# Weight means moved from ScalarE to VectorE and into the attention stage, and the softmax epilogue spread over the next tile

## The chip, the cores and the metric

One Trainium2 chip, all 8 cores, one launch. Two cores share one sequence of the batch of four: each computes 2048 of its 4096 rows of the output (blocks of 512 rows, taken alternately), and repeats the keys and values of the whole sequence for itself. There is no exchange between cores. The metric is the device time of the slowest core, in microseconds (us).

## What is computed

A pre-norm transformer layer on x of 4 x 4096 x 2048: `x1 = x + Attention(LN(x))`, then `x1 + FFN(LN(x1))`. Attention has 16 heads of 128, rotary positions and a causal mask. The FFN is a gated one with ternary weights:

```python
def _weight_quant(w):
    scale = jnp.clip(jnp.mean(jnp.abs(w)), EPS, None)
    wq = jnp.clip(jnp.round(w / scale), -1.0, 1.0) * scale
    return w + jax.lax.stop_gradient(wq - w)
...
gate = _bitlinear(x, w_gate)
up = _bitlinear(x, w_up)
return _bitlinear(jax.nn.silu(gate) * up, w_down)
```

What matters here is `mean(abs(w))` of three weight matrices of 64 MB each. A whole matrix must be read for its mean before its first element can be quantized, so the kernel reads 192 MB for the three means, long before the FFN reads the same matrices again.

## The kernel before

Each of the five engines (TensorE = PE, VectorE = DVE, ScalarE = ACT, GpSimd = POOL, SyncE = SP) works through its own list of instructions in order; the lists are recorded in program order and replayed (`Rec.replay`, so that every instruction of the trace carries line 68). A DMA sits in the list of the engine that issues it. Where an instruction waits for a semaphore, everything behind it in that engine's list waits too. The helpers `vop`, `sop` and `gop` also make each operation wait for the one before it on its own engine.

The stages, one after the other, with a barrier of all engines between them:

1. Rotary tables and the first layer norm. 2. Projections of q, k and v. 3. Attention (`with ExitStack() as p2`). 4. Output projection, x1 and the second norm (`p3`). 5. Gate and up matmuls with ternarizing (`p4`). 6. Down matmul (`p4e`).

**The weight means** (`wa_chunk`, L566). The 192 MB are cut into 192 chunks of 128x2048 f32 (1 MB). A chunk is loaded by a DMA that POOL issues into one of two tiles, `wa_t0` and `wa_t1`; POOL waits until the chunk that was in the tile before has been read. ACT then runs `Abs` over the chunk with its sum accumulated into `wa_tmp`, and a second instruction of one column adds that to `wa_acc`. `wa_feed(n)` (L592) puts n chunks at the place where it is called: 6 behind each of the 16 heads (L815), 4 in each of the 16 tiles of the output projection (L893), and 2 in each of the 16 tiles of the second pass over x1 (L937). `wa_epilogue` (L597), behind that pass, turns the three sums into the thresholds that stage 5 needs.

**Attention.** A head has four query tiles of 512 (`t`), and tile t has K_t = 8(t+1) key blocks of 128 (`kb`), 80 blocks in all. For each block PE makes the scores (`pb <- p_qT,p_kT`) in one of three PSUM banks, ACT the exponential into `p_E`, and DVE multiplies the last eight blocks of each tile by the mask. `drain` (L751) then adds the block to the row sums (`p2S <- p_E,g_ones_colb`) and to the context (`pb <- p_E,p_v`, in pb2 or pb3 by the parity of t); it runs three blocks behind the scores. `p2S` is one bank for all tiles. At the end of each tile the list reads:

```python
while pending2:
    p_ = pending2.pop(0)
    drain(p_, p_[0] == 0)
avdone = (sT, sT.v)
wait(V, avdone, (sV, sV.v))
vop("reciprocal", invr[:], p2S[0:1, :])
```

so the three blocks that are left are drained first. Then follow the reciprocal of the row sums on one partition (DVE), its broadcast to 128 partitions by an f32 matmul (PE, `p2A`), the copy out of PSUM (ACT, `p_bcb`), the product with the context (DVE, `p_ctx`) and the store (issued by ACT). I call these five the tile's epilogue. The first score matmuls of the next tile stand behind the broadcast on PE, and its first exponential stands behind the store on ACT.

**Between two heads.** At the end of head h stand 6 chunks on ACT (L815). At the start of head h+1 `load_head` (L661) has SP load q, k and v of head h+2 (2.5 MB, into the tiles that head h has given up), and `normB` (L681) makes the bound that head h+2 subtracts in its exponentials: DVE squares q and k (`p_dump`), PE sums them over the partitions in 12 matmuls, DVE takes 12 maxima (`p_nm`), and ACT, DVE and PE combine them into `p_negB`. The scores of head h+1 stand behind all of that in PE's list.

**Output projection** (L850). For each of 16 tiles of 128 rows: 64 matmuls in four PSUM banks, 8 DVE additions, then on ACT the store of x1 and two passes with accumulated sums (`p_dump`), then on DVE two reductions for the largest and the smallest value (`p_sw`), which wait for ACT's passes. The second pass (L920) loads x1 again and quantizes it with five DVE operations a tile.

Of the kernel before, what the change touches and what calls it, by code (L numbers as in the profile page):

```python
# [84 lines left out]
def build_program(upto=99):  # L85
# [535 lines left out]
    with ExitStack() as p2:  # L621
# [117 lines left out]
        for h in range(NH):  # L739
# [27 lines left out]
            pending2 = []  # L767
            for t in range(4):
                K_t = 8 * (t + 1)
                for kb in range(K_t):  # L770
# [21 lines left out]
                    pending2.append((kb, t, etok))  # L792
                while pending2:
                    p_ = pending2.pop(0)
                    drain(p_, p_[0] == 0)
                avdone = (sT, sT.v)
                wait(V, avdone, (sV, sV.v))
                vop("reciprocal", invr[:], p2S[0:1, :])
                p2rel[0] = (sV, sV.v)
                wait(T, p2Arel[0], (sV, sV.v))  # L800
                top("matmul", p2A[:], g_ones_row[:], invr[:], start=True, stop=True)
                wait(Sc, (sT, sT.v))
                sop("activation", bcb[:], p2A[:], AF.Identity)
                p2Arel[0] = (sS, sS.v)
                cb = t % 2
                wait(V, (sS, sS.v), ctxrel[cb])
                vop("tensor_tensor", ctxb[cb][:], pb[2 + t % 2][:], bcb[:], ALU.mult)
                prel[2 + t % 2] = (sV, sV.v)
                wait(Sc, (sV, sV.v))
                csem[cb].inc(Sc.dma_start(  # L810
                    d_ctxT.ap()[h * 128:(h + 1) * 128, t * 512:(t + 1) * 512],
                    ctxb[cb][:]), 16)
# [534 lines left out]
```

How the kernel before makes its waits and increments, by code:

```python
    def then_inc(self, sem, val=1):  # L46
        self.incs.append((sem, val))
        return self
# [17 lines left out]
    def replay(self, eng):  # L66
        for meth, a, k, inst in self.ops:
            real = getattr(eng, meth)(*a, **k)
            for sem, val in inst.incs:
                real.then_inc(sem, val)
# [8 lines left out]
    def inc(self, inst, n=1):  # L79
        inst.then_inc(self.h, n)
        self.v += n
        return self.v
# [62 lines left out]
    def wait(rec, *toks):  # L145
        for sem, val in toks:
            if val > 0:
                rec.wait_ge(sem.h, val)
# [1 line left out]
    def barrier_all():  # L150
        for r in RECS:
            for s in sems:
                if s.v > 0:
                    r.wait_ge(s.h, s.v)
# [39 lines left out]
    def vop(meth, *a, **k):  # L194
        if sV.v:
            V.wait_ge(sV.h, sV.v)
        return sV.inc(getattr(V, meth)(*a, **k))
# [1 line left out]
    def sop(meth, *a, **k):  # L199
        if sS.v:
            Sc.wait_ge(sS.h, sS.v)
        return sS.inc(getattr(Sc, meth)(*a, **k))
# [1 line left out]
    def gop(meth, *a, **k):  # L204
        if sG.v:
            G.wait_ge(sG.h, sG.v)
        return sG.inc(getattr(G, meth)(*a, **k))
```

## Time and profile before

| what | value |
|---|---|
| median of 2 runs | 10006.01 us (9992.61 to 10019.41) |
| profiled execution, its own time | 10008.06 us |
| its span, slowest core (core 2) | 10006.5 us |
| spans of the 8 cores | 9926.9 to 10006.5 us |
| mean granted TensorE clock, cores 0 to 3 / 4 to 7 | 0.813 / 0.783 |
| busy share of core 2: PE, DVE, ACT, POOL | 60%, 42%, 23%, 14% |
| attention stage, core 2 | about 2434 to 4727 us |
| output projection and second pass, core 2 | about 4728 to 5376 us |

The profile is one execution, read on its slowest core. Busy time is per engine; a stage in which no engine is near full is one in which they wait for each other in turn, and only the timeline tells in which order. In the timeline a row is start, duration, engine, instruction with output and inputs, and in brackets how long its engine stood idle before it and which engine or DMA ended that.

### The profile page before, as it was taken

The numbers are of one execution on the slowest core, as the hardware profiler recorded it, in microseconds if no ns is written. First come the engines' busy times: TensorE is split into PE (matmuls) and PEld (weight loads), VectorE is DVE, ScalarE is ACT, GpSimd is POOL, SyncE is SP. The second block draws the span as 40 slices with busy tenths as digits, with TensorE's granted clock in tenths as the row PEclk, the third lists the DMA queues.
The fourth block names the chain that finished last, engine by engine and source line by source line (L and its number), as shares of the span: only waits on it lengthen the run. The fifth ranks groups of instructions, "written<-read, shape, count | busy, mean of one in ns | idle before, by whom it ended". The sixth has DMA issues, their size and how long they took to land.

```text
span 10006.5 us, 90582 instructions; the slowest of 8 cores (9926.9 to 10006.5 us)
## 1 busy us (share of the span) xinstructions
PE 6033.1 (60%) x23243; PEld 2298.0 (23%) x23698; DVE 4159.0 (42%) x4832; ACT 2311.2 (23%) x3870; POOL 1371.6 (14%) x770
## 2 busy tenths in 40 slices
PE   0006476497766667665630678878779717484847
PEld 0002122143111111111210233333333313232323
DVE  5503233222333323331353677777776451514140
ACT  3531011000555555454451000000000110101010
POOL 0001122100000000000001433333333100000101
PEclk9999799798777777777865899999998757575868
DMA  2483321332122211222886444444444123333433
GB/s 88 145 290 76 67 51 50 66 74 75 40 76 76 76 58 58 76 76 64 268 285 199 128 127 125 126 127 126 122 126 125 61 74 131 104 135 102 144 107 133
DMA packets 637658, 1115.46 MB, mean 111 GB/s; under 512 B 339954, under 2 KB 421874, under 8 KB 567282
## 3 DMA queue, kind: packets, MB, share of 16 engines
q1 hardware_dynamic: 433380, 530.71, 17.6%
q10 hardware_dynamic: 158976, 302.06, 9.4%
q0 software_dynamic: 44816, 276.88, 9.1%
q8 instruction: 224, 3.67, 0.2%
q14 instruction: 262, 2.15, 0.1%
HBM read 874.62 MB, written 218.10 MB: 109 GB/s over the span
## 4 chain that ended last, share of the span: by engine, by line
PE 32%; DVE 29%; DMA 11%; ACT 8%; issue 7%; POOL 6%; SPq 3%; ACTq 2%; DVEq 1%; another core or an unknown queue 1%; POOLq 0%
PE pb L68 25%; DVE p_cu L68 5%; PE p2S L68 4%; SPq L68 3%; DVE p_hqt L68 3%; DVE t_w L68 3%; DMA wa_t<-wdT 3%; POOL p_wdtb L68 3%; ACTq L68 2%; DVE p_wf L68 2%; DVE p_pm L68 2%; DVE p_invr L68 2%; ACT wa_dump L68 2%; DMA wa_t<-wuT 2%; DVE p_ht L68 2%
## 5 line engine op out<-in xcount | busy, mean ns | idle before, releaser
L68 PE MATMUL pb<-p_wgt,p_xiT 128*128 128x512 bf16 x4014 | 1080.0, 427 | 604.1 <-DVE p_ht L68 415.1
L68 PE MATMUL pb<-p_wds,p_hTg 128*128 128x512 bf16 x4009 | 1018.1, 421 | 101.6 <-DMA p_wds<-wdtd 85.3
L68 ACT ACTIVATE p_E<-pb,p_negB 128x512 bf16<-128x512 f32 x1280 | 879.8, 687 | 351.3 <-PE pb L68 118.9
L68 DVE TENSOR_TENSOR p_cu<-g_sxinv,p4a_swn 128x1 f32<-128x1 f32 x256 | 753.8, 2945 | 27.8 <-DVE p_cg L68 1.5
L68 PEld LDWEIGHTS pb<-p_wgt,p_xiT 128*128 128x128 bf16 x4096 | 430.0, 107 | 1235.9 <-issue 930.8
L68 ACT ACTIVATE p_sg<-pb,p_cg 128x512 f32<-128x512 f32 x256 | 175.9, 687 | 2211.3 <-DVE p_cu L68 1288.5
L68 DVE TENSOR_TENSOR p_E<-p_E,p_masks 128x512 bf16<-128x512 bf16 x512 | 218.0, 426 | 1056.2 <-ACT p_E L68 1054.7
L68 PE MATMUL pb<-k_pp_xT,k_pp_W 128*128 128x512 bf16 x2007 | 467.0, 384 | 297.8 <-ACT k_pp_qb L68 193.3
L68 PE MATMUL pb<-p_qT,p_kT 128*128 128x512 bf16 x1222 | 535.9, 455 | 138.5 <-ACT p_E L68 126.5
L68 PE MATMUL ptb<-g_ident,p_hqo 128*128 128x128 bf16 x1024 | 127.4, 299 | 787.1 <-DVE p_hqo L68 642.7
L68 PEld LDWEIGHTS pb<-p_wds,p_hTg 128*128 128x128 bf16 x4096 | 432.4, 106 | 683.5 <-issue 499.6
L68 PE MATMUL pb<-q_pp_xT,q_pp_W 128*128 128x512 bf16 x1003 | 230.7, 382 | 543.9 <-DMA q_pp_xT<-xlnq 456.6
L68 DVE TENSOR_SCALAR p_hqt<-p_hq,p_st 128x1024 f32<-128x1024 f32 x128 | 97.3, 760 | 1047.1 <-PE ptb L68 911.2
L68 PE MATMUL p2S<-p_E,g_ones_colb 128*1 128x512 bf16 x1280 | 523.5, 409 | 11.3 <-ACT p_E L68 3.7
L68 PE MATMUL pb<-p_E,p_v 128*128 128x512 bf16 x1258 | 528.2, 420 | 0.0
L68 PE MATMUL pb<-v_pp_W,v_pp_xT 128*128 128x512 bf16 x2007 | 442.1, 380 | 105.5 <-DMA v_pp_xT<-xlnkv 103.4
L68 PE MATMUL p4b<-p_wut,p_xiT 128*128 128x512 bf16 x2007 | 474.9, 388 | 2.4
L68 PE MATMUL pb<-p_wut,p_xiT 128*128 128x512 bf16 x2007 | 473.7, 387 | 2.4
L68 ACT ACTIVATE wa_dump<-wa_t 128x2048 f32<-128x2048 f32 x192 | 366.7, 1910 | 447.5 <-DMA wa_t<-wdT 167.6
L68 POOL TENSOR_TENSOR p_wdtb<-p_wf,p_pm 128x2048 bf16<-128x2048 f32 x64 | 289.7, 4526 | 785.7 <-DVE p_wf L68 754.0
L68 POOL TENSOR_TENSOR p_ob<-p_ev,p_x1i 128x512 f32<-128x512 f32 x64 | 90.9, 1420 | 2014.0 <-ACT p_ev L68 1929.9
L68 PE MATMUL pb<-p_Wo,p_ct 128*128 128x512 bf16 x1003 | 248.6, 410 | 176.1 <-DVE p_x L68 87.6
(169 smaller groups left out, 6799.3 us busy)
## 6 DMA issues: line engine op xcount, KB each, us to landing
wa_t<-wgT POOLq DMA_DIRECT2D x64, 1024.0 KB, 6.1
wa_t<-wuT POOLq DMA_DIRECT2D x64, 1024.0 KB, 6.7
wa_t<-wdT POOLq DMA_DIRECT2D x64, 1024.0 KB, 8.2
p_wf<-wdT SPq DMA_DIRECT2D x64, 1024.0 KB, 5.7
p_wf<-wgT SPq DMA_DIRECT2D x64, 1024.0 KB, 5.8
p_wf<-wuT SPq DMA_DIRECT2D x64, 1024.0 KB, 5.4
hfpd<-p_ht ACTq DMA_DIRECT2D x256, 256.0 KB, 3.1
p_wds<-wdtd SPq DMA_DIRECT2D x64, 1024.0 KB, 6.5
```

What stands on the lines that cost most here:

```text
L68: real = getattr(eng, meth)(*a, **k)
```

## The change

Four edits:

- `wa_chunk`: the sum of absolute values of a chunk is made by DVE (`tensor_reduce` with absolute values, then an addition of one column), no longer by ACT. Each chunk also waits for all earlier DVE work. The tile `wa_dump` is gone.
- The chunks behind a head become 12 instead of 6. With 16 heads these are all 192, so that none are left in stage 4; `wa_feed` is taken out of both its passes, and `wa_epilogue` moves to the start of stage 4, behind the issue of the load of Wo.
- The three blocks left over at the end of a tile are drained only for the last tile of a head. For the others they stay in `pending2` and are drained between the first scores of the next tile.
- The epilogue of a tile becomes four functions e1 (reciprocal), e2 (broadcast), e3 (copy) and e4 (product and store), of which one is called at each of the key blocks 3, 4, 5 and 6 of the next tile. For the last tile of a head that is the first tile of the next head, behind the 12 chunks and `normB`.

```diff
@@ wa_chunk
-        toks = [(sem, sem.v)]
+        toks = [(sem, sem.v), (sV, sV.v)]
...
-        sop("activation", wa_dump[:, :W], wa_tile[slw][:, :W], AF.Abs,
-            accum_out=wa_tmp[:])
-        wa_state["rel"][slw] = (sS, sS.v)
-        sop("activation", wa_acc[mi][:], wa_tmp[:], AF.Identity,
-            bias=wa_acc[mi][:], scale=1.0)
+        wait(V, *toks)
+        vop("tensor_reduce", wa_tmp[:], wa_tile[slw][:, :W], AX.X, ALU.add,
+            apply_absolute_value=True)
+        wa_state["rel"][slw] = (sV, sV.v)
+        wait(V, (sV, sV.v))
+        vop("tensor_tensor", wa_acc[mi][:], wa_acc[mi][:], wa_tmp[:], ALU.add)
@@ attention, for each key block
                     qk_tok = sT.v
+                    if kb >= 3 and eitems:
+                        eitems.pop(0)()
                     while len(pending2) >= 3:
@@ attention, at the end of each tile
-                while pending2:
-                    p_ = pending2.pop(0)
-                    drain(p_, p_[0] == 0)
...
+                def mk_epi(h, t, cb):
+                    def e1():
+                        wait(V, (sT, sT.v), (sV, sV.v))
+                        vop("reciprocal", invr[:], p2S[0:1, :])
+                        p2rel[0] = (sV, sV.v)
+                    def e2():
+                        wait(T, p2Arel[0], (sV, sV.v))
+                        top("matmul", p2A[:], g_ones_row[:], invr[:],
+                            start=True, stop=True)
...
+                if t == 3:
+                    while pending2:
+                        p_ = pending2.pop(0)
+                        drain(p_, p_[1])
+                eitems.extend(mk_epi(h, t, t % 2))
             hrel[sl] = (sT, sT.v)
-            wa_feed(6)
+            wa_feed(12)
@@ stage 4
+        wa_feed(len(wa_items))
+        wa_epilogue()
...
-            wa_feed(4)
...
-            wa_feed(2)
-        wa_feed(len(wa_items))
-        wa_epilogue()
```

Where e1 stands, its wait `(sT, sT.v)` counts the scores of key block 3, which PE has just been given; the drain behind it starts the row sums of the new tile in `p2S` and waits for the reciprocal (`p2rel`).

DVE's list between heads 0 and 1, before: the last masked block of head 0, its reciprocal and context, then the squares and maxima of `normB(2)`.

```order
L68 TENSOR_TENSOR p2_E7<-p2_E7,p2_masks 128x512
L68 RECIPROCAL p2_invr<-p2S 1x512
L68 TENSOR_TENSOR p2_ctx1<-pb3,p2_bcb 128x512
L68 TENSOR_TENSOR p2_dump<-p2_qT0 128x2048
L68 TENSOR_REDUCE p2_nm0<-pb5 1x1
L68 TENSOR_TENSOR p2_dump<-p2_kT0 128x4096
L68 TENSOR_REDUCE p2_nm2<-pb0 1x1
```

DVE's list at the same place now, from the last two chunks on. Ten more pairs like these stand ahead of them, behind the last masked block; `wa_t0` and `wa_t1` are the two chunk tiles.

```order
L68 TENSOR_REDUCE wa_tmp<-wa_t0 128x1
L68 TENSOR_TENSOR wa_acc0<-wa_acc0,wa_tmp 128x1
L68 TENSOR_REDUCE wa_tmp<-wa_t1 128x1
L68 TENSOR_TENSOR wa_acc0<-wa_acc0,wa_tmp 128x1
L68 TENSOR_TENSOR p2_dump<-p2_qT0 128x2048
L68 TENSOR_REDUCE p2_nm0<-pb5 1x1
L68 TENSOR_TENSOR p2_dump<-p2_kT0 128x4096
L68 TENSOR_REDUCE p2_nm2<-pb0 1x1
```

The reciprocal and the context of head 0's last tile are no longer here, and `normB(2)` stands behind twelve chunks.

DVE's list a little later, at the start of head 1:

```order
L68 TENSOR_TENSOR p2_E0<-p2_E0,p2_masks 128x512
L68 TENSOR_TENSOR p2_E1<-p2_E1,p2_masks 128x512
L68 TENSOR_TENSOR p2_E2<-p2_E2,p2_masks 128x512
L68 RECIPROCAL p2_invr<-p2S 1x512
L68 TENSOR_TENSOR p2_E3<-p2_E3,p2_masks 128x512
L68 TENSOR_TENSOR p2_E4<-p2_E4,p2_masks 128x512
L68 TENSOR_TENSOR p2_E5<-p2_E5,p2_masks 128x512
L68 TENSOR_TENSOR p2_ctx1<-pb3,p2_bcb 128x512
L68 TENSOR_TENSOR p2_E6<-p2_E6,p2_masks 128x512
L68 TENSOR_TENSOR p2_E7<-p2_E7,p2_masks 128x512
L68 RECIPROCAL p2_invr<-p2S 1x512
```

The reciprocal at the fourth row belongs to the last tile of head 0, and so does `p2_ctx1`; the one at the end belongs to the first tile of head 1.

PE's list from the first tile of head 0 into the second, before: the last two blocks are drained, the broadcast follows, then four score matmuls (into pb0, pb1, pb4, pb0) before the first drain of the new tile.

```order
L68 MATMUL p2S<-p2_E6,g_ones_colb 1x512
L68 MATMUL pb2<-p2_E6,p2_v0 128x512
L68 MATMUL p2S<-p2_E7,g_ones_colb 1x512
L68 MATMUL pb2<-p2_E7,p2_v0 128x512
L68 MATMUL p2A<-p2_invr,g_ones_row 128x512
L68 MATMUL pb0<-p2_qT0,p2_kT0 128x512
L68 MATMUL pb1<-p2_qT0,p2_kT0 128x512
L68 MATMUL pb4<-p2_qT0,p2_kT0 128x512
L68 MATMUL pb0<-p2_qT0,p2_kT0 128x512
L68 MATMUL p2S<-p2_E0,g_ones_colb 1x512
L68 MATMUL pb3<-p2_E0,p2_v0 128x512
```

And now, from the same drains on:

```order
L68 MATMUL p2S<-p2_E6,g_ones_colb 1x512
L68 MATMUL pb2<-p2_E6,p2_v0 128x512
L68 MATMUL pb4<-p2_qT0,p2_kT0 128x512
L68 MATMUL p2S<-p2_E7,g_ones_colb 1x512
L68 MATMUL pb2<-p2_E7,p2_v0 128x512
L68 MATMUL pb0<-p2_qT0,p2_kT0 128x512
L68 MATMUL p2S<-p2_E0,g_ones_colb 1x512
L68 MATMUL pb3<-p2_E0,p2_v0 128x512
L68 MATMUL pb1<-p2_qT0,p2_kT0 128x512
L68 MATMUL p2A<-p2_invr,g_ones_row 128x512
L68 MATMUL p2S<-p2_E1,g_ones_colb 1x512
L68 MATMUL pb3<-p2_E1,p2_v0 128x512
```

The drains of the old tile stand between the scores of the new one. The reciprocal runs on DVE between the scores into pb0 and the drain of `p2_E0` that follows them; the broadcast stands one block later.

## Rows read from the trace of the kernel before

**Rows 1.** DVE timeline, the last two reciprocals of one head and the first of the next: start us, us, engine, instruction, [idle before <-releaser]
```profile
2720.91 3.35 DVE L68 RECIPROCAL p_invr<-p2S 1x512 f32<-1x512 f32 x1 [1.19 <-PE pb L68]
...
2758.64 3.35 DVE L68 RECIPROCAL p_invr<-p2S 1x512 f32<-1x512 f32 x1 [1.19 <-PE pb L68]
...
2805.39 3.35 DVE L68 RECIPROCAL p_invr<-p2S 1x512 f32<-1x512 f32 x1 [1.19 <-PE pb L68]
```

**Rows 2.** ACT timeline inside a tile in steady running, one of 1280 exponentials
```profile
2604.36 0.69 ACT L68 ACTIVATE p_E<-pb,p_negB 128x512 bf16<-128x512 f32 x1 [0.16 <-ACT p_E L68]
```

**Rows 3.** PE timeline, the broadcast matmul behind a reciprocal
```profile
2584.77 2.04 PE L68 MATMUL p2A<-p_invr,g_ones_row 1*128 1x512 f32 x2 [3.74 <-DVE p_invr L68]
```

**Rows 4.** windows after it: stretch, us, busy PE, PEld, DVE, ACT, POOL, PEclk, DMA share, GB/s
```profile
2584.80:2588.30 3.50, 3.40 (x5) 0.72 (x5) 0.50 (x1) 0.60 (x1) 0.00 (x0) 0.50 0.00 0
...
2594.20:2598.00 3.80, 3.64 (x14) 0.88 (x14) 0.00 (x0) 2.96 (x5) 0.00 (x0) 1.00 0.00 0
```

**Rows 5.** timeline of the boundary between two heads, all engines
```profile
2768.97 0.53 POOL L68 DMA_DIRECT2D wa_t<-wgT  x1 [116.22 <-ACT wa_acc L68]
...
2772.19 1.23 DVE L68 TENSOR_TENSOR p_dump<-p_qT 128x2048 bf16<-128x2048 bf16 x1 [6.34 <-DMA p_kT<-kTd]
...
2777.30 1.91 ACT L68 ACTIVATE wa_dump<-wa_t 128x2048 f32<-128x2048 f32 x1 [6.02 <-DMA wa_t<-wgT]
...
2790.45 0.15 DVE L68 TENSOR_TENSOR p_nm<-p_nm 1x1 f32<-1x1 f32 x1
...
2791.74 0.55 ACT L68 ACTIVATE p_nm<-p_nm 1x1 f32<-1x1 f32 x2
...
2793.94 0.27 PEld L68 LDWEIGHTS pb<-p_qT,p_kT 128*128 128x128 bf16 x2
...
2796.64 0.59 PE L68 MATMUL p2S<-p_E,g_ones_colb 128*1 128x512 bf16 x1 [0.19 <-issue]
```

**Rows 6.** timelines of DVE, ACT and POOL behind the last head, where no head is loaded
```profile
4697.35 3.35 DVE L68 RECIPROCAL p_invr<-p2S 1x512 f32<-1x512 f32 x1 [1.19 <-PE pb L68]
...
4704.64 0.33 ACTq L68 DMA_DIRECT2D ctxTd<-p_ctx  x1
...
4707.67 0.53 POOL L68 DMA_DIRECT2D wa_t<-wuT  x1 [112.96 <-ACT wa_acc L68]
...
4715.34 0.53 POOL L68 DMA_DIRECT2D wa_t<-wuT  x1 [4.65 <-ACT wa_acc L68]
...
4726.17 0.29 ACT L68 ACTIVATE wa_acc<-wa_tmp,wa_acc 128x1 f32<-128x1 f32 x1
```

**Rows 7.** DVE timeline, output projection, from its first tile's reduction to its last
```profile
4813.53 2.29 DVE L68 TENSOR_REDUCE p_sw<-p_x 128x1 f32<-128x2048 f32 x1 [4.91 <-ACT p_dump L68]
...
4818.45 0.69 DVE L68 TENSOR_TENSOR p_x<-pb,g_bob 128x512 f32<-128x512 f32 x1 [0.17 <-DVE p_sw L68]
...
5168.93 0.18 DVE L68 TENSOR_SCALAR p_sw<-p_sw 128x16 f32<-128x16 f32 x1 [11.39 <-ACT wa_acc L68]
```

**Rows 8.** DVE timeline, second pass over x1, first two tiles and the end
```profile
5179.21 1.34 DVE L68 TENSOR_SCALAR p_tq<-p_x,p_sw 128x2048 f32<-128x2048 f32 x1 [5.25 <-DMA p_x<-x1d]
...
5188.26 1.34 DVE L68 TENSOR_SCALAR p_tq<-p_x,p_sw 128x2048 f32<-128x2048 f32 x1 [0.25 <-DVE p_xi L68]
...
5376.14 0.16 DVE L68 RECIPROCAL p4a_invtau<-p4a_tau 128x1 f32<-128x1 f32 x1 [1.61 <-ACT p4a_tau L68]
```

**Rows 9.** windows, the output projection: columns as in rows 4
```profile
4790.00:5169.00 379.00, 248.51 (x1003) 105.50 (x1022) 161.81 (x161) 211.11 (x256) 33.52 (x64) 0.83 0.86 282
```

**Rows 10.** POOL, DVE and ACT timelines, a chunk issued beside a DVE reduction
```profile
4952.59 2.29 DVE L68 TENSOR_REDUCE p_sw<-p_x 128x1 f32<-128x2048 f32 x1 [0.17 <-DVE p_sw L68]
4952.61 0.53 POOL L68 DMA_DIRECT2D wa_t<-wuT  x1 [6.36 <-ACT wa_acc L68]
...
4960.21 1.91 ACT L68 ACTIVATE wa_dump<-wa_t 128x2048 f32<-128x2048 f32 x1 [1.24 <-DMA wa_t<-wuT]
```

**Rows 11.** DMA issues of the third weight matrix: xcount, KB each, median us to landing
```profile
wa_t<-wdT POOLq DMA_DIRECT2D x64, 1024.0 KB, 8.2
```

More of the change, by code:

```diff
@@ L599, in wa_epilogue @@
             b_swn, b_tau, b_invtau = wstats[mi]
-            wait(T, prel[5], (sS, sS.v))
+            wait(T, prel[5], (sS, sS.v), (sV, sV.v))
             top("matmul", pb[5][0:1, 0:1], wa_acc[mi][:], g_ones_col[:],
@@ L675, in build_program @@
         Erel = [(sS, 0)] * NEB
+        pending2 = []
+        eitems = []
         ctxrel = [(dm["c0"], 0), (dm["c1"], 0)]
@@ L751, in drain @@
             def drain(pend, first_sum):
-                pkb, pt, etok = pend
+                pkb, pt, etok = pend[0] if isinstance(pend[0], tuple) else pend
                 eb = pkb % NEB
@@ L765, in drain @@
                 Erel[eb] = (sT, sT.v)
-            pending2 = []
             for t in range(4):
@@ L791, in build_program @@
                         etok = (sV, sV.v)
-                    pending2.append((kb, t, etok))
-                while pending2:
-                    p_ = pending2.pop(0)
[L795 to L812, printed above, removed]
@@ L813, in build_program, with e3, e4 @@
-                ctxrel[cb] = (csem[cb], csem[cb].v)
-            hrel[sl] = (sT, sT.v)
-            wa_feed(6)
+                    pending2.append(((kb, t, etok), kb == 0))
+                def mk_epi(h, t, cb):
[7 more added lines that the diff above has]
+                            start=True, stop=True)
+                    def e3():
+                        wait(Sc, (sT, sT.v))
+                        sop("activation", bcb[:], p2A[:], AF.Identity)
+                        p2Arel[0] = (sS, sS.v)
+                    def e4():
+                        wait(V, (sS, sS.v), ctxrel[cb])
+                        vop("tensor_tensor", ctxb[cb][:], pb[2 + t % 2][:],
+                            bcb[:], ALU.mult)
+                        prel[2 + t % 2] = (sV, sV.v)
+                        wait(Sc, (sV, sV.v))
+                        csem[cb].inc(Sc.dma_start(
+                            d_ctxT.ap()[h * 128:(h + 1) * 128,
+                                        t * 512:(t + 1) * 512], ctxb[cb][:]), 16)
+                        ctxrel[cb] = (csem[cb], csem[cb].v)
+                    return [e1, e2, e3, e4]
@@ L816, in build_program @@
+                if t == 3:
+                    while pending2:
+                        p_ = pending2.pop(0)
+                        drain(p_, p_[1])
+                eitems.extend(mk_epi(h, t, t % 2))
+            hrel[sl] = (sT, sT.v)
+            wa_feed(12)
+        while pending2:
+            p_ = pending2.pop(0)
+            drain(p_, p_[1])
+        while eitems:
+            eitems.pop(0)()
         barrier_all()
```

2 lines of the change are left out of this document (removed).

## The prediction

> **What bounds the kernel now.** I read the views in this order: the spans of all cores (within 80 us of each other, no exchange between them, so core 2 stands for all), the busy shares (no engine near full, so the stages are chains of waits), and then the timelines of the two stages that the change touches.
>
> Attention first. The reciprocal of row sums marks the end of a tile. Between the third and the fourth of a head lie 37.7 us [rows 1], for 32 key blocks. In steady running a block takes 0.69 + 0.16 = 0.85 us [rows 2], so the blocks account for 27.0 and the tile boundary for 10.7 us; the shorter tiles leave the same remainder. In it PE stands idle for 3.7 us until the reciprocal is done, then needs 2.0 us for the broadcast [rows 3], waits again for the copy, the product and the first exponential, and runs at the lower of its two clocks meanwhile: granted 0.50 (1.2 GHz), back at 1.00 (2.4 GHz) some 10 us after the reciprocal began [rows 4].
>
> From the last reciprocal of a head (call it R, 2758.64) to the next head's first scores lie 35.3 us [rows 1, 5]. Two chains run side by side there: on ACT the six weight chunks, on DVE the squares and maxima of the norm bound, 2772.19 to 2790.60, 18.4 us. They end together (ACT's logarithms start at 2791.74), and the scores follow 2.2 us later [rows 5]. Today the means are thus nearly hidden beside the norm.
>
> A chunk's cost is its load, not its arithmetic: two tiles, each on a cycle of load, read, release. Undisturbed, the cycle is 4707.67 to 4715.34 = 7.7 us for a tile, thus two chunks [rows 6]. Beside the head's own load the landing grew to 8.3 us, from 2768.97 to 2777.30 [rows 5].
>
> In the output projection the core moves 282 GB/s [rows 9], and ACT's chunks stand between DVE's additions and its reductions. In the first tile no chunk stood there, and DVE waited 4.91 us for ACT [rows 7].
>
> **The change part by part.**
>
> (a) *Boundary with a norm, 14 of them.* All twelve chunks now stand in DVE's list, and the norm's DVE work, 18.4 us, stands behind them. What was side by side becomes a sum. The first chunk can start when the last mask is done, R - 1.1 (the reciprocal's idle time [rows 1]). A chunk costs DVE its reduction of 128x2048, 2.29 us by the same operation [rows 7], plus about 0.4 for the addition and two gaps: 2.7. Release to reissue took ACT 2.56 us (7.67 less a landing of 5.1 there); with the longer reduction I take 2.84. The first two chunks are already loaded. The load into the second tile is issued at 2.7 + 2.84 = 5.5, lands after 8.3 under the head load at 13.8, and four more cycles bring the twelfth chunk. Alone a cycle is 7.7 + 0.28 = 7.95; I take 8.2, as the head load is still draining. 13.8 + 32.8 + 2.7 = 49.3. Then the norm 18.4 and ACT's and PE's 2.3: scores at R - 1.1 + 49.3 + 18.4 + 2.3 = R + 68.9, for R + 35.3. That is +33.6 each, +470 in all. Queued behind the waiting DVE are the masks of the new head, and behind `normB` PE's scores, so nothing else fills the gap.
>
> (b) *The boundary into head 15* has no norm and no head load. ACT's six chunks end there today at about R + 29 (the same pattern as in [rows 6]); DVE's twelve end at R - 1.1 + (5.5 + 5.1 + 4 x 7.95 + 2.7 = 45.1) = R + 44. Scores and exponentials run ahead, the first mask waits: +14.
>
> (c) *End of attention.* Today the last chunk is done at 4726.46 = R + 29.1. Then: chunks until R + 44.0, behind them the last epilogue, which took 4697.35 to 4704.97 = 7.6 us: R + 51.6, so +22 [rows 6].
>
> (d) *Tile boundaries inside a head, 48.* The flush is gone; PE still stops once, between the scores of block 3 and the drain that needs `p2S` free. What stands behind the wait is everything on PE, and nothing covers it: 3.7 us. The broadcast adds 2.0 at the lower clock, and two groups of matmuls at half speed another 1.2; then the clock is back. Copy, product and store lie beside PE's work, since ACT has 0.16 us free per block and PE is three blocks ahead. 3.7 + 2.0 + 1.2 = 6.9 for 10.7: -3.8 each, -182. The bounds: 4.6 (clock stays up, broadcast in 0.85) and 8.8 (ACT's and DVE's parts, 1.9, not hidden).
>
> (e) *The epilogue of each head's last tile* now falls in the next head's first tile, 15 times. Today the first row sum there comes 2.7 us after the scores, at 2796.64 [rows 5]. It will wait for three exponentials and masks (some 3.8 us) and the reciprocal behind them, 3.35: 4.6 later. With the broadcast, 2.0, less 1.4 since fewer groups then run at half clock: +5.2, in all +78. Bounds 0 and 7.5.
>
> (f) *Output projection.* Without chunks a tile costs DVE 8 additions of 0.69 + 0.17 = 6.92, the wait of 4.91, and 4.92 for two reductions: 16.75 us. PE was busy 248.5/16 = 15.5 us a tile [rows 9] and stays inside. From 4818.45 fifteen tiles end at 5069.7, for 5168.93: -99 [rows 7]. Two chunk loads less beside the load of Wo: -3 (0 to -7).
>
> (g) *Second pass.* A tile without chunk traffic takes 5188.26 - 5179.21 = 9.05 us; 16 are 144.8, with the last store about 5 more: 5329 for 5376.3, -47 [rows 8]. The weight epilogue of 8 us is hidden beside the Wo load; uncovered it would cost those 8.
>
> Sum: 470 + 14 + 22 - 182 + 78 - 99 - 3 - 47 = +253. Against the profiled execution's own 10008 us that gives 10261; the median of the runs lies 2 us lower, so I forecast 10260 us. In a sentence: 96 chunks leave a place where each cost 1.5 us and enter one where each costs 4, with the norm no longer beside them.
>
> **The rivals.**
>
> *Not slower: the chunk chain runs at DVE's pace.* If loads kept ahead of 2.7 us a chunk, twelve would take 32.4 us: -16.9 in 14 places, -12.7 in two, -262 in all, 9999 us. Speaking for it: DVE itself has only 2.7 us of work a chunk. Against: ten loads in 24 us are some 430 GB/s, and the core moved 282 GB/s in its densest stretch [rows 9]. To come back within 2% the cycle would have to fall to 7.3 us, below the undisturbed 7.7.
>
> *The clock stays up in the short stops.* Then a tile boundary costs 4.6 and the head start 1 less: -125, 10136 us, within 2%. Against: the broadcast ran at 0.50 straight after a stop of the same 3.7 us [rows 3, 4]. For: before that stop the engine was fully busy and now it is again soon after.
>
> *Loads land as in the projection stage.* Median 8.2 us there [rows 11], with the neighbour cores loading too. A cycle of 11.0: +2.8 for 56 cycles and +3.1 for 8, 10445 us. For: bursts now fill 70 of some 167 us of a head instead of 35 of 140, so neighbours meet more often. Against: the other traffic of the core, which made up a third of those bytes, is absent.
>
> *POOL cannot write descriptors while DVE reduces.* ACT never stood in POOL's way; DVE might. If each reissue waited for one reduction, 64 x 2.29 = 147 us more: 10408. Against: a chunk issued 0.02 us after a DVE reduction had begun was in use 7.6 us later, less than the median of 8.2 [rows 10, 11]. The Trainium skill (SBUF — State Buffer, "SBUF: two separate sides") warns of this trap for DVE operations in a two-port mode, whose lock keeps POOL from writing the descriptors of its own DMAs; its section "Who interferes with whom" says that on trn2 a `tensor_reduce` has no such mode and never contends. By that rule this rival falls away, and the trace agrees with the 7.6 us.
>
> **How the numbers follow.** Forecast 0.72, DVE's pace 0.04, clock up 0.09, slow landings 0.10, descriptors 0.05. The forecast's own range takes the cycle (7.5 to 9.0: -45 to +50), the tile boundary (6 to 8: -43 to +53), head start and projection (16 to 18.5 us a tile), and some 40 us for stages 5 and 6, which the change does not touch but whose cores drift against each other by 80 us: 10170 to 10370. The 8-in-10 range reaches to the clock rival below and toward the two slow ones above: 10140 to 10410. A change of 2%, 200 us, is about what a measurement of this kernel can tell; slower than 10206 is most of the forecast (0.63) and the two slow rivals: 0.78. Within 2%: the lower tail of the forecast and the first two rivals, 0.21. Faster: 0.01.
>
> **What would show it.** Right: from a head's last mask to the next head's scores about 70 us with DVE idle on `wa_t` loads between reductions of 2.3 us; `p_dump` only behind the twelfth; head period about 167 us for 140; reciprocals with PE idle 3.7 us and a broadcast at clock 0.50; the projection's reductions every 16.8 us; attention some 400 us longer per core and stage 4 some 150 shorter. Wrong: `p_dump` beside chunks, chunk cycles under 7 us, tile boundaries as long as before, or a projection tile still near 21 us, which would mean that PE or the x loads bound it.

## The result, and the profile after

The changed kernel takes 10480.47 us (median of 11 runs, 10436.47 to 10517.63), the kernel before 9969.39 us beside it (10 runs, 9896.47 to 10023.9): a ratio of 1.052, 95% interval 1.049 to 1.056. It is slower, as forecast, but by 511 us where 253 were forecast, and its time lies above the range. The profiled execution took 10464.24 us. Here and below, ratios and their intervals use only executions in which no die of the chip ran visibly slower than in the others; the medians given hold all executions.

Spans of the cores after. Core 6 is the slowest now; I read core 2 in both kernels, so that like stands beside like. Attention grew by 608 us on core 6 and by 621 on core 2.

```profile
core 2: 10377.9 us, clock 0.812
...
core 6: 10462.6 us, clock 0.798
```

**Between two heads.** DVE timeline of the same boundary as in [rows 5] (start us, us, engine, instruction, idle before and releaser):

```profile
2799.56 2.29 DVE L68 TENSOR_REDUCE wa_tmp<-wa_t 128x1 f32<-128x2048 f32 x1 [0.18 <-DVE p_E L68]
...
2811.49 2.29 DVE L68 TENSOR_REDUCE wa_tmp<-wa_t 128x1 f32<-128x2048 f32 x1 [6.51 <-DMA wa_t<-wgT]
...
2846.76 2.29 DVE L68 TENSOR_REDUCE wa_tmp<-wa_t 128x1 f32<-128x2048 f32 x1 [2.04 <-DMA wa_t<-wgT]
...
2850.64 2.29 DVE L68 TENSOR_REDUCE wa_tmp<-wa_t 128x1 f32<-128x2048 f32 x1 [1.27 <-DMA wa_t<-wgT]
...
2853.51 1.23 DVE L68 TENSOR_TENSOR p_dump<-p_qT 128x2048 bf16<-128x2048 bf16 x1 [0.24 <-DVE wa_acc L68]
...
2871.43 0.15 DVE L68 TENSOR_TENSOR p_nm<-p_nm 1x1 f32<-1x1 f32 x1
...
2877.93 3.35 DVE L68 RECIPROCAL p_invr<-p2S 1x512 f32<-1x512 f32 x1 [0.17 <-DVE p_E L68]
```

And POOL's issues of the loads there:

```profile
2802.41 0.53 POOL L68 DMA_DIRECT2D wa_t<-wgT  x1 [131.06 <-DVE wa_acc L68]
2805.20 0.53 POOL L68 DMA_DIRECT2D wa_t<-wgT  x1 [2.27 <-DVE wa_acc L68]
...
2840.91 0.53 POOL L68 DMA_DIRECT2D wa_t<-wgT  x1 [3.63 <-DVE wa_acc L68]
```

The order of events is the forecast one: twelve chunks, of which every one from the third waits for its load, then the 18 us of the norm, then the new head, with the old head's reciprocal behind its first three masks. The twelve took 2799.56 to 2853.26 = 53.7 us, for 49.3 forecast. The cycle of one tile is release 2.84 us (2838.07 to 2840.91) and landing 5.85 (2840.91 to 2846.76) = 8.7, not 8.2; the first two loads, beside the head's load, took 9.1 (2802.41 to 2811.49) and 10.6. Over the 14 boundaries with a norm the twelve chunks took 54.4 us in the mean, so this one is typical.

**Inside a head.** Timelines of DVE, ACT and PE from tile 1 to tile 2 at a reciprocal, answering to [rows 3]:

```profile
2737.00 3.35 DVE L68 RECIPROCAL p_invr<-p2S 1x512 f32<-1x512 f32 x1 [2.85 <-PE pb L68]
2737.01 0.69 ACT L68 ACTIVATE p_E<-pb,p_negB 128x512 bf16<-128x512 f32 x1 [0.16 <-ACT p_E L68]
...
2740.59 0.59 PE L68 MATMUL p2S<-p_E,g_ones_colb 128*1 128x512 bf16 x1 [3.84 <-DVE p_invr L68]
...
2742.07 2.07 PE L68 MATMUL p2A<-p_invr,g_ones_row 1*128 1x512 f32 x2
2742.41 0.69 ACT L68 ACTIVATE p_E<-pb,p_negB 128x512 bf16<-128x512 f32 x1 [4.71 <-PE pb L68]
...
2745.78 0.60 ACT L68 ACTIVATE p_bcb<-p2A 128x512 f32<-128x512 f32 x1 [2.68 <-PE pb L68]
...
2746.47 0.69 ACT L68 ACTIVATE p_E<-pb,p_negB 128x512 bf16<-128x512 f32 x1
...
2747.03 0.38 PE L68 MATMUL p2S<-p_E,g_ones_colb 128*1 128x512 bf16 x1
...
2747.39 0.69 DVE L68 TENSOR_TENSOR p_ctx<-pb,p_bcb 128x512 bf16<-128x512 f32 x1 [7.05 <-ACT p_E L68]
...
2748.16 0.33 ACTq L68 DMA_DIRECT2D ctxTd<-p_ctx  x1
...
2748.76 1.47 ACT L68 ACTIVATE p_E<-pb,p_negB 128x512 bf16<-128x512 f32 x2 [1.60 <-PE pb L68]
...
2749.89 0.38 PE L68 MATMUL pb<-p_qT,p_kT 128*128 128x512 bf16 x1 [0.47 <-ACT p_E L68]
```

The windows over it (columns as in [rows 4]):

```profile
2740.50:2743.00 2.50, 2.41 (x4) 0.70 (x5) 0.00 (x0) 0.59 (x1) 0.00 (x0) 0.50 0.00 0
2743.00:2747.00 4.00, 4.00 (x8) 0.42 (x6) 0.00 (x0) 1.23 (x3) 0.00 (x0) 0.50 0.02 4
2747.00:2750.00 3.00, 2.53 (x10) 0.66 (x9) 0.69 (x1) 1.30 (x3) 0.00 (x0) 1.00 0.12 44
```

PE stops for 3.84 us behind the reciprocal, works until 2747.03 at 0.50 (1.2 GHz), three groups of matmuls and the broadcast, and is back at 1.00. But ACT's column shows what I had hidden: its list holds the copy `p_bcb`, one exponential, and then the store, for which it waits until DVE has made `p_ctx`. Between 2737.01 and 2748.76 ACT begins three exponentials, 11.75 us for what steady running does in 2.5.

Part of this is not the epilogue's work but how its waits are written. The broadcast has ended at 2744.14, yet the copy starts at 2745.78, released by `PE pb`: e3 waits for PE's latest count, which holds the scores that were put into PE's list just before it. In the same way `p_ctx` is released by `ACT p_E` (2747.39), an exponential later than the copy that it needs (ended 2746.38). Together that is some 2.3 us at this boundary in which ACT or DVE waits for work whose result it does not use; no experiment narrowed these two waits.

**At the start of a head**, PE and ACT:

```profile
2874.38 1.06 PE L68 MATMUL pb<-p_qT,p_kT 128*128 128x512 bf16 x2 [0.33 <-issue]
...
2881.53 0.58 PE L68 MATMUL p2S<-p_E,g_ones_colb 128*1 128x512 bf16 x1 [5.02 <-DVE p_invr L68]
```
```profile
2883.35 0.69 ACT L68 ACTIVATE p_E<-pb,p_negB 128x512 bf16<-128x512 f32 x1 [5.47 <-PE pb L68]
2886.72 0.60 ACT L68 ACTIVATE p_bcb<-p2A 128x512 f32<-128x512 f32 x1 [2.68 <-PE pb L68]
...
2890.58 1.47 ACT L68 ACTIVATE p_E<-pb,p_negB 128x512 bf16<-128x512 f32 x2 [2.48 <-PE pb L68]
```

The first row sum stands 7.15 us behind the first score matmul. Counted from that matmul's weight load (2873.98), as the 2.7 us of before were, it is 7.55 us.

**Stage 4 and the loads**, answering to [rows 7, 8, 11] and [rows 6]: DVE in the projection and at the start of the second pass; DVE behind the last head; the loads' median (this row is core 6's; core 2 has 5.9).

```profile
5463.14 2.29 DVE L68 TENSOR_REDUCE p_sw<-p_x 128x1 f32<-128x2048 f32 x1 [4.91 <-ACT p_dump L68]
...
5479.71 2.29 DVE L68 TENSOR_REDUCE p_sw<-p_x 128x1 f32<-128x2048 f32 x1 [4.91 <-ACT p_dump L68]
...
5496.49 2.29 DVE L68 TENSOR_REDUCE p_sw<-p_x 128x1 f32<-128x2048 f32 x1 [4.91 <-ACT p_dump L68]
...
5720.85 0.17 DVE L68 TENSOR_SCALAR p_sw<-p_sw 128x16 f32<-128x16 f32 x1 [0.60 <-DVE p_sw L68]
...
5730.99 1.35 DVE L68 TENSOR_SCALAR p_tq<-p_x,p_sw 128x2048 f32<-128x2048 f32 x1 [5.12 <-DMA p_x<-x1d]
...
5873.20 2.29 DVE L68 TENSOR_TENSOR p_xi<-p_qi,p_tq 128x2048 bf16<-128x2048 int32 x1
```
```profile
5321.29 2.29 DVE L68 TENSOR_REDUCE wa_tmp<-wa_t 128x1 f32<-128x2048 f32 x1 [0.17 <-DVE p_E L68]
...
5367.38 2.29 DVE L68 TENSOR_REDUCE wa_tmp<-wa_t 128x1 f32<-128x2048 f32 x1 [0.87 <-DMA wa_t<-wdT]
```
```profile
wa_t<-wdT POOLq DMA_DIRECT2D x64, 1024.0 KB, 5.7
```

A projection tile takes 16.78 us (forecast 16.75). From the end of the first tile's two reductions (5463.14 + 4.92) to the row at 5720.85 DVE needs 253 us, for 350.5 in [rows 7]; the second pass ends 5873.20 + 2.29, 144.5 us behind its first operation. The last head's twelve chunks take 48.7 us (forecast 45.1, counted from one mask's end to the last sum).

### The profile page after: what moved, and what is told of

Same layout as the page of the kernel before. It is cut to its first block, busy times and chain, and to the rows that moved or that the text cites. A ratio compares the mean times of both kernels' runs of the same rounds, so it can differ in the third digit from the quotient of the medians.

```text
span 10462.6 us, 91232 instructions; the slowest of 8 cores (10357.9 to 10462.6 us)
## 1 busy us (share of the span) xinstructions
PE 6076.2 (58%) x23698; PEld 2285.4 (22%) x23698; DVE 4631.8 (44%) x5216; ACT 1869.8 (18%) x3294; POOL 1366.3 (13%) x770
## 4 chain that ended last, share of the span: by engine, by line
PE 33%; DVE 33%; DMA 10%; ACT 7%; issue 7%; POOL 5%; SPq 3%; ACTq 2%; DVEq 1%; another core or an unknown queue 1%; POOLq 0%
PE pb L68 26%; DVE p_cu L68 5%; PE p2S L68 4%; SPq L68 3%; DVE p_hqt L68 3%; DVE t_w L68 3%; POOL p_wdtb L68 3%; DVE wa_tmp L68 2%; DVE p_pm L68 2%; DVE p_wf L68 2%; DVE p_invr L68 2%; ACT p_E L68 2%; ACTq L68 2%; DMA wa_t<-wuT 2%; DMA wa_t<-wgT 2%
## 5 line engine op out<-in xcount | busy, mean ns | idle before, releaser
L68 PE MATMUL pb<-p_wds,p_hTg 128*128 128x512 bf16 x4096 | 917.8, 388 | 93.9 <-DMA p_wds<-wdtd 85.6
L68 PE MATMUL pb<-k_pp_xT,k_pp_W 128*128 128x512 bf16 x2048 | 510.1, 409 | 255.4 <-ACT k_pp_qb L68 152.7
L68 PE MATMUL pb<-p_dump,g_ones_colb 128*1 128x512 bf16 x192 | 107.2, 593 | 915.2 <-DVE p_dump L68 796.1
L68 DVE TENSOR_REDUCE wa_tmp<-wa_t 128x1 f32<-128x2048 f32 x192 | 438.9, 2286 | 359.1 <-DMA wa_t<-wuT 123.5
L68 PE MATMUL pb<-p_qT,p_kT 128*128 128x512 bf16 x1280 | 564.9, 446 | 37.6 <-ACT p_E L68 37.1
L68 PE MATMUL pb<-v_pp_W,v_pp_xT 128*128 128x512 bf16 x2048 | 515.0, 423 | 102.0 <-DMA v_pp_xT<-xlnkv 102.0
L68 PE MATMUL pb<-p_E,p_v 128*128 128x512 bf16 x1280 | 561.7, 439 | 0.0
L68 PE MATMUL pb<-q_pp_xT,q_pp_W 128*128 128x512 bf16 x1024 | 259.3, 416 | 517.8 <-DMA q_pp_xT<-xlnq 458.7
L68 PEld LDWEIGHTS pb<-p_wds,p_hTg 128*128 128x128 bf16 x4096 | 407.1, 100 | 601.7 <-issue 140.2
L68 POOL TENSOR_TENSOR p_wgt<-p_wf,p_pm 128x2048 bf16<-128x2048 f32 x64 | 288.7, 4510 | 407.9 <-DVE p_wf L68 392.7
```

The source lines that it names most:

```text
L68: real = getattr(eng, meth)(*a, **k)
```

## The experiments

Eleven kernels. The first four take the change apart, the next three each attack one loss of the changed kernel, the last four show what the two losses are worth together. Head periods are those of core 2, from one head's `p_dump<-p_qT` to the next: 139.1 us before at the same place, 182.7 after. All ratios are to the kernel before on the same chip, whose median moved from chip to chip (9967.7 to 10002.8 us). The changed kernel was not run again beside them, so a difference to it compares medians that were not taken side by side; where it matters I give the attention stage of the traces as well, 2798.4 us in the changed kernel and 2177.4 before (core 2, first to last exponential).

**1. The epilogue alone.** The kernel before with only the third and fourth edit; chunks stay on ACT, 6/4/2.

```diff
-                while pending2:
-                    p_ = pending2.pop(0)
-                    drain(p_, p_[0] == 0)
...
+                eitems.extend(mk_epi(h, t, t % 2))
```

Expected: 

> Only the epilogue edit: chunks stay on ScalarE, 6 behind a head, 4 and 2 in stage 4. Theory A (tile boundaries gain 1.0 us where 3.8 was forecast, and the last tile's epilogue costs the next head what its absence gives the boundary): within 60 us of before, tile boundaries near 9.7 us. Rival B (the epilogue edit itself is a loss and carries the missing 230 us): 100 to 230 us slower than before. The forecast's own term would give 100 us or more faster.

Measured: 9936.4 us for 10002.8, ratio 0.995 (0.990 to 1.000); head period 137.6. The edit by itself wins half a per cent, some 50 to 66 us, at the edge of what the interval tells. Attention on core 2 took 2140.4 us, 37 less than before. So the 182 us that I had credited to the tile boundaries are not there.

**2. The engine alone.** Chunks on DVE, still 6/4/2, old epilogue.

```diff
-        wait(Sc, *toks)
-        sop("activation", wa_dump[:, :W], wa_tile[slw][:, :W], AF.Abs,
-            accum_out=wa_tmp[:])
+        wait(V, *toks)
+        vop("tensor_reduce", wa_tmp[:], wa_tile[slw][:, :W], AX.X, ALU.add,
+            apply_absolute_value=True)
```

Expected: 

> Only the engine: chunks on VectorE, still 6, 4 and 2, old epilogue. Theory A (the norm's VectorE work can no longer run beside the chunks): a head boundary of about R + 62 instead of R + 35, 14 times, +375; the projection's tiles +4 each and the second pass +2 each, +100; in all about 475 us slower. Rival B (what costs is only that more chunks stand in attention): within 100 us of before.

Measured: 10440.3 us (4 runs), ratio 1.046 (1.037 to 1.056). The head period is 159.6, 20.5 more, with no chunk added: about the norm's 18.4 us, which have left their place beside the chunks. In stage 4, from the first projection matmul to the last `p_xi`, 758 us stand for 554: DVE has 96 chunks more to do there. That the total, +437, came near the 475 expected is partly luck: a boundary was put at +27 and cost 20.5, stage 4 was put at +100 and cost 204.

**3. Engine and place.** As 2, with `wa_feed(12)` behind each head and none in stage 4.

```diff
-            wa_feed(6)
+            wa_feed(12)
```

Expected: 

> Engine and placement, old epilogue: chunks on VectorE, 12 behind each head, none in stage 4. Theory A: as the changed kernel, plus 48 tile boundaries of 1 us: 500 to 570 us slower than before. Rival B (epilogue edit a loss): 300 to 400 slower.

Measured: 10543.0 us, ratio 1.058 (1.050 to 1.066); head period 185.2. To the whole change (1.052) only the epilogue edit is missing: again about half a per cent, less than the interval; the head period agrees, 185.2 for 182.7.

**4. The place alone.** Twelve chunks behind each head on ACT, none in stage 4, old epilogue.

Expected: 

> Only the placement: chunks stay on ScalarE, 12 behind each head, none in stage 4, old epilogue. Theory A: the norm stays hidden beside the chunks, a boundary grows by six chunks of 4.2 us, 16 x 25 = +400, stage 4 gives back 150: about 250 us slower. Rival B (placement alone explains the result): 450 us or more slower.

Measured: 10243.9 us, ratio 1.026 (1.017 to 1.035); head period 164 to 168. Six chunks more are three cycles of a tile, 25 us. The parts add up: 20.5 for the engine and 25 to 29 for the place, 46 for both.

**5. Score banks.** The changed kernel; the three PSUM banks are taken in turn across tiles, so that the last block of a tile and the first of the next never share one.

```diff
-                    bank = SCB[kb % 3]
+                    bank = SCB[scc[0] % 3]
+                    scc[0] += 1
```

Expected: 

> The changed kernel with the three score banks taken in turn across tiles (before: block 15 of tile 1 and block 0 of tile 2 share a bank). Theory A (part of the missing gain at a tile boundary is this wait for an exponential, 0.7 us of PE and 1.0 of ACT in the trace, at the one boundary of a head where both blocks have one bank): the boundary from tile 1 to 2 shorter by 0.7 to 1 us, 10 to 30 us off the changed kernel. Rival B: no boundary shorter.

Measured: 10439.3 us (2 runs), ratio 1.049 (1.039 to 1.060); tile 1 to tile 2 takes some 22 us for 23.4. The collision is real in the trace; the gain in time is smaller than the interval.

**6. Three chunk tiles.** The changed kernel with `wa_t2` added.

```diff
-    wa_tile = [sba(f"wa_t{i}", [128, 2048], F32) for i in range(2)]
+    wa_tile = [sba(f"wa_t{i}", [128, 2048], F32) for i in range(3)]
...
-        slw = i % 2
+        slw = i % 3
```

Expected: 

> The changed kernel with three chunk tiles instead of two. Theory A (a chunk's price is the cycle of load, reduction and release, 4.35 us with two tiles): twelve chunks in about 45 us instead of 53.7, 16 x 8 = 130 us off the changed kernel. Rival B (the loads are bound by what the core or its neighbours can move): the twelve chunks take as long as before, within 40 us of the changed kernel. Rival C (VectorE hinders POOL's descriptors): landings stay near 5.5 us and nothing is gained either.

The first and the last chunk of a boundary, DVE, and windows in the middle of the chunks, here and in the changed kernel (columns as in [rows 4]):

```profile
2790.79 2.29 DVE L68 TENSOR_REDUCE wa_tmp<-wa_t 128x1 f32<-128x2048 f32 x1 [0.18 <-DVE p_E L68]
...
2831.54 2.29 DVE L68 TENSOR_REDUCE wa_tmp<-wa_t 128x1 f32<-128x2048 f32 x1 [0.95 <-DMA wa_t<-wgT]
...
2806.00:2834.00 28.00, 0.00 (x0) 0.00 (x0) 19.86 (x18) 0.00 (x0) 4.23 (x8) 0.50 1.00 349
```
```profile
2822.00:2852.00 30.00, 0.00 (x0) 0.00 (x0) 17.41 (x15) 0.00 (x0) 3.70 (x7) 0.50 0.71 245
```

Measured: 10293.1 us (3 runs), ratio 1.034 (1.023 to 1.044). The twelve take 43.4 us for 53.7, some 190 us off the whole kernel (attention on core 2 is 179 us shorter). With two tiles the chain was their cycle, not the loads' rate: the DMA engines were busy 0.71 of the time, at 245 GB/s, and one more load in flight shortens it by a fifth. With three tiles it is the rate: busy 1.00, 349 GB/s, and the landings of `wgT` grew from 5.9 to 8.0 us. A fourth tile would thus not be expected to help; it was not tried.

**7. Two row sums.** The changed kernel; even tiles sum in the sixth bank, odd ones in `p2S`, so no drain waits for a reciprocal.

```diff
-                top("matmul", p2S[0:1, :], g_ones_colb[:], Eb[eb][:],
+                top("matmul", (pb[5] if pt % 2 == 0 else p2S)[0:1, :], g_ones_colb[:], Eb[eb][:],
```

Expected: 

> The changed kernel with the row sums of even tiles in bank 5 and of odd ones in p2S, so that no drain waits for a reciprocal. Theory A (most of a tile boundary's remaining 9.3 us is PE's stop of 3.8 us for the reciprocal, and the lower clock behind it): tile boundaries of 1.5 to 4 us, 48 x 6 = 290 us off the changed kernel, and the head start 4 us shorter, 60 more. Rival B (ScalarE's wait for the product and its store issue take the stop's place): boundaries of 5 to 7 us, 150 us off.

PE and ACT behind a head start and behind its first tile:

```profile
2877.72 2.04 PE L68 MATMUL p2A<-p_invr,g_ones_row 1*128 1x512 f32 x2 [3.81 <-DVE p_E L68]
...
2894.29 1.09 PE L68 MATMUL p2A<-p_invr,g_ones_row 1*128 1x512 f32 x2 [2.89 <-DVE p_invr L68]
```
```profile
2885.26 1.47 ACT L68 ACTIVATE p_E<-pb,p_negB 128x512 bf16<-128x512 f32 x2 [2.48 <-DVE p_ctx L68]
```

Measured: 10306.2 us (2 runs), ratio 1.036 (1.025 to 1.047), 174 us off by the medians; attention is shorter by 84 us on core 2 and by 96 to 135 on the others. That is theory B's size or less, and well short of A's 290. The wait for the reciprocal did not go; it moved one block on, from the row sum to the broadcast, which stands in the same list and needs the same result. At a head start the broadcast even waits for the mask behind the reciprocal (`DVE p_E`), since it waits for DVE's latest count. Behind it ACT still waits for the context.

**8. Chunks between key blocks.** The changed kernel, with one chunk behind each of twelve key blocks of a head.

```diff
+            SPR = [(7, 0), (7, 1), (15, 1), (7, 2), (11, 2), (15, 2), (23, 2), (7, 3),
+                   (11, 3), (15, 3), (19, 3), (23, 3)]
...
+                    if (kb, t) in SPR:
+                        wa_feed(1)
...
-            wa_feed(12)
```

Expected: 

> The changed kernel with its twelve chunks of a head on VectorE spread over the key blocks of the tiles, none at the head's end. Theory A (what costs is that the chunks stand between the last mask and the norm, not that VectorE does them): a head boundary of about 29 us from the last reciprocal to the next scores, no chunk wait left, 150 to 230 us faster than the kernel before. Rival B (the chunks' VectorE time or their DMA traffic slows the tiles): each chunk costs the tiles its 2.7 us, 192 x 2.7 = 520 more, 300 us slower than before.

DVE in a long tile, and at the head's end:

```profile
2756.66 2.29 DVE L68 TENSOR_REDUCE wa_tmp<-wa_t 128x1 f32<-128x2048 f32 x1 [4.01 <-DMA wa_t<-wgT]
...
2782.24 1.23 DVE L68 TENSOR_TENSOR p_dump<-p_qT 128x2048 bf16<-128x2048 bf16 x1 [7.66 <-DMA p_kT<-kTd]
```

Measured: 9868.7 us (5 runs), ratio 0.988 (0.979 to 0.997). Some 600 us are gone, and the kernel is faster than the one before by 1.2%, clear of no change but with an interval that reaches from 0.3 to 2.1%. The 108 us between the medians are less than the 150 forecast; the interval holds both. What is left shows in the trace. Blocks ahead of the last eight of a tile have no mask, so nothing in DVE's list lies between their chunks: the first two of the long tile ran back to back (2747.24 and 2750.03), the third waited 4.01 us for its load, and the mask behind the fifth began at 2767.39, 4.1 us behind its exponential. At the head's end DVE waits for the next head's load.

**9. The epilogue late.** The changed kernel with two row sums (as 7), banks in turn (as 5), e1 to e4 at 3, 7, 8 and 9 blocks, and the store issued by SP. These are four edits at once; what each gives beyond experiments 5 and 7 was not taken apart.

```diff
-                    if kb >= 3 and eitems:
-                        eitems.pop(0)()
+                    while eitems and eitems[0][0] <= blk[0]:
+                        eitems.pop(0)[1]()
...
-                        csem[cb].inc(Sc.dma_start(
+                        csem[cb].inc(Y.dma_start(
...
+                eitems.extend([(blk[0] + 1 + p_, f_) for p_, f_ in
+                               zip(EPOS, mk_epi(h, t, t % 2))])
```

Expected: 

> Everything of the changed kernel, with four edits at the tile boundary: the row sums of even and odd tiles have two places, the four epilogue steps come 3, 7, 8 and 9 key blocks into the next tile instead of at once, SyncE and not ScalarE issues the store of the context tile, and the score banks are used in turn across tiles. Theory A (the 9.7 us left at each tile boundary is the stop for the row sum, the half clock behind it and ScalarE's wait for the context and its store, all of which lie in the code's order): a boundary falls to 1 to 3 us, so 48 inside heads give 48 x 7 = 336 us and the 15 at head starts about as much each, 60 to 100 us: 350 to 430 us off the changed kernel, about 10050 to 10130. Theory B (something else, VectorE's masks or ScalarE's steps, is due there next): no more than the second row of sums alone gave, 174 us, about 10300.

The broadcast behind a reciprocal, PE:

```profile
2772.03 1.09 PE L68 MATMUL p2A<-p_invr,g_ones_row 1*128 1x512 f32 x2 [0.28 <-DVE p_invr L68]
```

Measured: 10078.7 us (4 runs) for 9967.7, ratio 1.012 (1.008 to 1.015), 402 us off the changed kernel, in the middle of theory A (attention on core 2 383 us shorter). Four blocks between reciprocal and broadcast cover it: PE waits 0.28 us instead of 3.84, the granted clock is 1.00 from the first reciprocal of a head to the third in 15 of 16 heads (0.78 to 0.88 in the changed kernel), and 16 and 24 blocks take 15.5 and 21.7 us from reciprocal to reciprocal, for 23.4 and 28.7. The head period is 157.5 us, for 182.7.

**10. Both losses.** As 9, with three chunk tiles, nine chunks between key blocks and three at the head's end.

```diff
+            SPR = [(7, 0), (15, 1), (8, 2), (12, 2), (23, 2), (8, 3), (12, 3),
+                   (16, 3), (20, 3)]
...
-            wa_feed(12)
+            wa_feed(3)
```

Expected: 

> As i_late, and the twelve chunks of a head are reduced between the key blocks (nine inside the tiles, three at the head's end), from three chunk tiles instead of two. Theory A (the two losses are separate: the chunks' chain ahead of the norm, and the boundary of the tiles): a head is its key blocks (some 102 us), its tile boundaries (3 x 2) and a boundary between heads of about 29 us, near 135 us for 182, so 15 x 45 = 680 us or more off the changed kernel: 9650 to 9800, faster than the kernel before by 2 to 4%. Theory B (VectorE with masks, reductions and epilogue is the bound of a head once nothing else waits): no faster than the spread chunks alone, 9869.

Windows of one head on core 2: its tiles, the boundary, the first tile of the next (columns as in [rows 4]):

```profile
2612.00:2684.00 72.00, 66.73 (x211) 14.46 (x214) 42.51 (x46) 49.27 (x73) 4.78 (x9) 0.91 0.40 138
2684.00:2716.00 32.00, 10.69 (x24) 2.29 (x24) 21.63 (x34) 1.79 (x6) 1.59 (x3) 0.58 0.57 180
2716.00:2727.00 11.00, 7.72 (x16) 1.49 (x16) 7.98 (x10) 5.11 (x8) 0.00 (x0) 0.66 0.01 1
```

Measured: 9437.6 us (4 runs) for 9967.7, ratio 0.948 (0.943 to 0.954): 10% under the changed kernel and 5% under the one before. The head period is 115 us. That is 200 us better than I had allowed. An error of mine stands behind it: the 102 us that I put down for the key blocks already held three old tile boundaries, as 80 blocks of 0.85 are 68 us. Inside the tiles PE is busy 66.7 of 72 us; what is left is the boundary, 32 us at mean clock 0.58.

**11. The norm between key blocks.** As 10, with the norm cut into queued steps (square, matmul, maximum and so on, 31 in all), one behind a key block, in `p2A`. The chunks stand elsewhere too: eleven between key blocks and one at the head's end, for nine and three.

```diff
-                normB(h + 1)
+                nlist.extend(norm_steps(h + 1))
...
+                    if not fired and t and kb < 8 * t:
+                        norm_one()
```

Expected: 

> As k_best, but the next head's norm is computed in small steps between key blocks instead of behind the last tile, and eleven chunks are spread with one at the head's end. Theory A (the serial norm, about 28 us of small VectorE and TensorE steps in a row at each of 14 boundaries, is what is left between heads): 200 to 390 us less than k_best. Theory B (those steps stop TensorE in its order or load VectorE as they stand between key blocks): what is won at the boundary is lost in the tiles, the time within 100 us of k_best.

Two of its matmuls, PE:

```profile
2671.33 0.59 PE L68 MATMUL p2A<-p_dump,g_ones_colb 128*1 128x512 bf16 x1 [5.88 <-DVE p_dump L68]
...
2699.32 0.58 PE L68 MATMUL p2A<-p_dump,g_ones_colb 128*1 128x512 bf16 x1 [2.92 <-DVE p_nm L68]
```

Measured: 9488.6 us (4 runs), ratio 0.952 (0.949 to 0.956), theory B. The last tile with its boundary falls from 61.3 to 38.3 us, but the two tiles before it grow from 16.5 to 26.3 and from 24.2 to 38.1. The rows show how: a norm matmul in PE's list waits 2.9 or 5.9 us for a step that DVE has only just been given, and all scores stand behind it. That a placement with several blocks between the partners, as in 9, would keep the gain was not tried.

## Why the prediction was right in sign and wrong in size

Core 2, each term of the sum beside what the trace shows:

| term | forecast | measured | from |
|---|---|---|---|
| (a) 14 boundaries with norm | +470 | +543 | first chunk to scores, mean of the 14: 75.3 us for 36.5, 38.8 each (38.0 at the one shown) |
| (b) into head 15 | +14 | about +16 | reciprocal of tile 2 to that of the next tile 0, 78.0 to 100.1 us, less (e) and (d) |
| (c) end of attention, with the -3 for the load of Wo | +19 | +26 | last exponential to first projection matmul, 95.1 to 121.2 us |
| (d) 48 tile boundaries | -182 | -52 | head 0, first exponential to the end of its last mask: 100.1 to 96.9 us, x16 |
| (e) last epilogue in the next head | +78 | +111 | the same stretch, mean of heads 1 to 14 over head 0: 8.9 us more, for 1.4 before; x15 |
| (f, g) stage 4 | -146 | -147 | first projection matmul to DVE's last work, 586.4 to 434.5 us, with 5 us for the last store |

They sum to +497. Attention as a whole, first to last exponential, grew from 2177 to 2798 us on core 2, by 621; its terms (a, b, d, e) account for 618 of them. The terms of (d) and (e) together are a loss here, though experiment 1 showed a small gain for the same edit: the epilogue of a head's last tile has also left the boundary, and that gain lies in (a).

*Right.* The mechanism of (a): the norm no longer runs beside the chunks, and more chunks stand there. Experiments 2 and 4 show the two halves apart, 20.5 and 25 to 29 us a head, and experiment 8 shows the chain's share by taking it out. Right to the microsecond was the projection (16.75 forecast, 16.78), and the second pass.

*The step that failed* is (d): "Copy, product and store lie beside PE's work, since ACT has 0.16 us free per block and PE is three blocks ahead." They do not. A tile boundary costs 8.4 to 9.9 us, not 6.9: the stop 3.84, three groups at half clock instead of two (1.9 for 1.2), the broadcast 2.0, and then ACT's wait for the context and its store, because PE's lead of three blocks had been eaten by the very stop in front of it, and because the waits of copy and product count more than they need; at one boundary in a head the shared score bank adds PE 0.7 and ACT 1.0 us. I had named 8.8 as the bound, with 1.9 us for ACT's and DVE's parts, and then counted those parts as hidden. Experiment 9 bears the cause out: with these waits taken out, by distance, a second place for the row sums, banks in turn and SP's store together, 402 us go. That is the largest error, 130 us. (e) fits the same cause: its stop was nearly right (7.55 us from the weight load to the first row sum, 7.3 forecast), and ACT's part behind it was missing; the 33 us were not split further.

*A term mis-sized:* (a) by 73 us. The chain is release plus landing of two tiles, as said, but the landing was 5.9 us and not 5.4, and two loads stand under the head's load, not one (9.1 and 10.6 us): 53.7 for 49.3. Experiment 6 confirms that with two tiles the cycle, not the rate, sets it. A slip of 1 us stands in (b): R + 44 less R + 29 is 15, not 14.

*What the sum does not hold.* It ends with stage 4. Over its whole span core 2 grew by only 371 us (10006.5 to 10377.9), since stages 5 and 6, which the change does not touch, took less on it (the first window is the kernel before, the second the changed one):

```profile
5377.00:10006.00 4629.00, 3113.80 (x13061) 1365.59 (x13312) 2361.31 (x2384) 422.39 (x1345) 994.10 (x321) 0.80 0.37 118
```
```profile
5876.00:10377.00 4501.00, 2978.23 (x13061) 1332.18 (x13312) 2366.11 (x2384) 422.36 (x1345) 994.21 (x321) 0.83 0.38 122
```

The 4629 us before are the exception: cores 0, 1 and 4 to 7 took 4480 to 4497 us there, core 3 4613, and after the change all eight took 4482 to 4527. The spans of the single cores grew by 371 to 495 us, the slowest span by 456 and the medians by 511. So a forecast built on one core's stages is good to some 100 us here. Why cores 2 and 3 were late before stays open; the granted clock alone does not tell it, as core 5 had 0.79 and took 4489 us. That the sum, 497, lies so close to the 511 of the medians is therefore in part luck.

*The rivals.* DVE's own pace (9999 us) fell: DVE waited for a load at ten of twelve chunks. "The clock stays up" fell: 0.50 behind the stop, as in [rows 4]. Landings as in the projection (8.2 us) fell: the median is 5.7 to 5.9 in the last matrix, so with 10445 us that rival came near the time for a wrong reason. POOL's descriptors fell too: POOL issued a load at 2802.41, 0.05 us after a reduction had begun, in 0.53 us. The Trainium skill (SBUF — State Buffer, "Who interferes with whom") says that a `tensor_reduce` never contends with GpSimd on trn2; the trace agrees, with the same 0.53 us that POOL takes when DVE is idle.

The head's load is issued by SP and the chunks by POOL, yet the first two chunks landed in 9.1 and 10.6 us and those behind the head's load in about 5.9. The Trainium skill (DMA: Bandwidth & Descriptors, "Issuing engines are not separate DMA queues") says that transfers run on the same 16 engines and interleave whichever engine started them; the trace agrees, in that SP's load slowed POOL's by 3.2 us and 4.7 us.
